# Coefficient loads reordered, down stages two slots later, and query products handled as pairs

## The chip, the cores and the metric

The kernel runs on one core of a Trainium2 chip. The metric is the time of one execution on the device in microseconds; times before are the median of three runs. One execution was also profiled, and all rows come from it. The page abbreviates the engines: PE is TensorE's products and PEld its weight loads, DVE is VectorE, ACT is ScalarE, POOL is GpSimd, SP is SyncE, and a q behind a name (SPq) is the engine's own instruction queue.

## What is computed

One transformer layer with linear attention and a butterfly feed-forward part, x being 4 x 1024 x 128 in fp32, with 16 heads of 64:

```python
qkv = x @ W_qkv                               # 128 -> 3 * 1024
fmap = lambda t: relu(t @ W_f + b_f)          # per head, 64 x 64
q, k = fmap(q), fmap(k)
kv = einsum('bhnd,bhne->bhde', k, v)
out = einsum('bhnd,bhde->bhne', q, kv)
normalizer = einsum('bhnd,bhd->bhn', q, k.sum(axis=2))
out = out / (normalizer[..., None] + 1e-06)
x = layernorm(x + out @ W_out + b_out)
h = butterfly(x @ W_exp + b_exp, up_weights, 512)       # 9 stages
h = butterfly(gelu(h + up_bias), down_weights, 512)     # 9 stages
x = layernorm(x + h @ W_con + b_con + down_bias)
```

A butterfly stage takes each pair of features whose indices differ in one bit and multiplies it by a 2 x 2 matrix of its own. All stages are linear, so the kernel applies them to the weights once and not to each token.

## The kernel before

Each engine runs a program of its own, with semaphores between them. After a prologue that loads and folds weights, the work is laid out over 48 slots (`for s in range(SLOTS)`, in every engine's program, and always in the order written there); what belongs to slot s is given by small tables and functions at the head of the kernel. An engine works through its own list in order, so an operation that waits holds up all behind it on that engine, the next slots too.

The main stream, in the order in which a unit goes through it:

- **k tiles** (`k_tiles`, 32 of 128 tokens: two a slot in slots 0 to 3, then one a slot to slot 27). TensorE projects a tile in two halves, ScalarE copies each through a ReLU into `k`, TensorE multiplies the tile with x (`add_kx`), and VectorE adds it to `k_total` (`k_sum`).
- **k sums**: after a batch's eight tiles TensorE reduces `k_total` over tokens (`ksum`, slots 6, 14, 22, 30) into the PSUM bank `desk`, and VectorE spreads the result by `ksum_mask` into `ksum_cols`, its first operation in that slot. All later transposes and head maps go through the same bank, so the next of them waits for that.
- **q products** (`q_steps`, 64 of 128x512, two a slot in slots 4 to 35): TensorE, then ScalarE's ReLU into the ring `q` of 16 (`q_relu`).
- **normalizers**: every 4th slot from 8 on, `norm` on TensorE, `norm_eps` on ScalarE, `reciprocal` on VectorE; SyncE's `spread(n)` then writes the reciprocals to DRAM and reads them back broadcast over partitions, in two halves, into `recips`. The first `spread` stands in SyncE's program behind all loads of coefficients.
- **normalised q** (`spreads`, two a slot in slots 10 to 41): VectorE multiplies q by the reciprocals (`normalise_q`, into `qn`, two buffers), ScalarE copies it in the reduced format fp32r (`qn_hi`, into `qn_h`), VectorE subtracts that copy for the low part (`qn_lo`, into `qn_l`); in the next slot TensorE adds the three products of `add_attn` (slots 11 to 42).
- **attention end**: `transpose_attn`, then in slots 15, 19, ... 43 VectorE's `add_x` and layer norm. GpSimd makes the reciprocal deviation (`rstd_of`), and VectorE's `layer_norm_end` waits for it.
- **feed-forward**: up products with GELU, `down`, `transpose_y`, and VectorE's `residual` with a second layer norm, in slots 22, 26, ... 42, 44, 47.

Beside that stream the two butterflies are applied to the weights. GpSimd does the nine up stages (`up_step`, on `y_up`) ahead of its slots, three operations each. VectorE does the nine down stages (`down_step`, on `y_dn`), two products and a sum each, stage n in slot 1 + n (`DOWN_STEP_SLOT`), as the last large operation of the slot; besides there are small stages for the biases (`bias_row_step`, slots 2 to 5). The results are wanted in slot 15. A stage's coefficients are 512 KB, broadcast to all partitions by SyncE's `load_up(n)` and `load_down(n)` into two buffers each. From n = 2 on a load waits for both products of stage n - 2 to be done (`s_up` or `s_dn` at 3n - 4), and SyncE issues all its transfers in order.

The lines of VectorE's slot that the change touches, of the kernel before:

```python
for a in spreads(s):
    normalise_q(a)
if s in NORM_SLOT:
    reciprocal(NORM_SLOT[s])
# xT_lo, x1T_lo, k_sum of this slot
for a in spreads(s)[:1]:
    qn_lo(a)
# add_x or residual of this slot, with the statistics of its layer norm
for a in spreads(s)[1:]:
    qn_lo(a)
# layer_norm_end, m_lo, down_step
```

Of the kernel before, what the change touches and what calls it, by code (L numbers as in the profile page):

```python
# [5 lines left out]
def postln_linear_attention_butterfly_ffn_kernel(  # L6
# [52 lines left out]
    QRING = 16  # L59
# [51 lines left out]
    WEIGHTS_SLOT = 15  # L111
    DOWN_STEP_SLOT = {1 + n: n for n in range(STAGES)}

# [48 lines left out]
    with ctx:  # L162
# [169 lines left out]
        def _(sp):  # L332
# [36 lines left out]
            load_up(0)  # L369
            load_down(0)  # L370
            sp.dma_start(xs[1][:, :, :], xs_view[1, :, :, :]).then_inc(s_xs[1], 16)
            load_down(1)
            load_up(1)
            sp.dma_start(coef_rows[:, :, :], up_weights[0:LOCAL, :, :, :].rearrange("s (a k) i j -> a s (k i j)", a=HT))\
                .then_inc(s_ccol, 16)
            for st in range(LOCAL, STAGES):
                sp.dma_start(coef_cols[:, st - LOCAL, :, :],
                             up_weights[st, :, :, :].rearrange("(m p) i j -> p m (i j)", p=128)).then_inc(s_ccol, 16)
            column(bout_col[:, :], b_out)
            column(bcon_col[:, :], b_con)  # L380
            column(bdn_raw[:, :], down_bias)
            for i in range(HT):
                column(bup_raw[:, i:i + 1], up_bias[i * 128:(i + 1) * 128])
            for n in range(2, STAGES):
                load_down(n)
                load_up(n)
                if n == 4:
                    for b in range(2, BATCH):
                        sp.dma_start(xs[b][:, :, :], xs_view[b, :, :, :]).then_inc(s_xs[b], 16)

            def spread(n):

                sp.wait_ge(s_r, n + 1)
                for j in range(4):
                    sp.dma_start(recip_rows[n, :, j * QT:(j + 1) * QT], recip[32 * j:32 * j + 2 * PAIRS, :])\
                        .then_inc(s_rst, 16)
                sp.wait_ge(s_rst, 64 * (n + 1))
                rows = recip_rows[n, :, :].rearrange("(o p h) t -> h o p t", o=1, h=2)
                for half in range(2):
                    g = 2 * n + half  # L400
                    if g >= 2:
                        sp.wait_ge(s_qn, RC * (g - 1))
                    for h in range(2):
                        sp.dma_start(recips[h * D:(h + 1) * D, half, :, :],
                                     rows[h, :, half * RC:(half + 1) * RC, :].to_broadcast([D, RC, CH]))\
                            .then_inc(s_rc[half], 16)
# [71 lines left out]
        def _(pe):  # L478
# [115 lines left out]
            def add_attn(a):  # L594
# [3 lines left out]
                if p == 0 and a:  # L598
                    pe.wait_ge(s_atc, a // PAIRS)
                pe.wait_ge(s_qnh, a + 1)  # L600
                pe.wait_ge(s_qnl, a + 1)
                split(attn_ps[:, :], (m_h[:, p, :], m_l[:, p, :]), (qn_h[:, a % NRING, :], qn_l[:, a % NRING, :]),
# [140 lines left out]
        def _(act):  # L743
# [17 lines left out]
            def q_relu(i):  # L761
                act.wait_ge(s_made, ring_of["q", i] + 1)
                if i >= QRING:
                    act.wait_ge(s_qn, i - QRING + 1)
                a_.activation(q[:, i % QRING, :], bank(("q", i))[:, :], ACT.Relu, bias=bf_col[:, :])\  # L765
                    .then_inc(s_taken, 1)

            def qn_hi(a):
                act.wait_ge(s_qn, a + 1)
                if a >= NRING:  # L770
                    act.wait_ge(s_at, a - NRING + 1)
                hi(qn_h[:, a % NRING, :], qn[:, a % 2, :], s_qnh)

# [69 lines left out]
            for s in range(SLOTS):  # L843
# [6 lines left out]
                if s == 0:  # L850
                    for half, fold in enumerate([attn_ps, spare_ps]):
                        act.wait_ge(s_fold, half + 3)
                        hi(wq_h[:, half * CH:(half + 1) * CH], fold[:, :], s_wh)
                for a in spreads(s)[:1]:
                    qn_hi(a)
                for i in q_steps(s)[:1]:
                    q_relu(i)
                for kt in k_tiles(s)[:1]:
                    k_relu(kt, 1)
                for a in spreads(s)[1:]:  # L860
                    qn_hi(a)
                for n in range(ALLCH):
# [34 lines left out]
        def _(dve):  # L897
# [91 lines left out]
            def normalise_q(a):  # L989
                if a % RC == 0:  # L990
                    dve.wait_ge(s_rc[a // RC % 2], 32 * (a // RC // 2 + 1))
                if a >= 2:
                    dve.wait_ge(s_qnh, a - 1)
                    dve.wait_ge(s_qnl, a - 1)
                v.tensor_tensor(qn[:, a % 2, :], q[:, a % QRING, :], recips[:, a // RC % 2, a % RC, :],  # L995
                                ALU.mult).then_inc(s_qn, 1)

            def qn_lo(a):
                dve.wait_ge(s_qnh, a + 1)
                lo(qn_l[:, a % NRING, :], qn[:, a % 2, :], qn_h[:, a % NRING, :], s_qnl)  # L1000

# [59 lines left out]
            for s in range(SLOTS):  # L1061
# [4 lines left out]
                if s == 0:  # L1066
                    for half, fold in enumerate([attn_ps, spare_ps]):
                        cols = slice(half * CH, (half + 1) * CH)
                        dve.wait_ge(s_wh, 3 + half)
                        lo(wq_l[:, cols], fold[:, :], wq_h[:, cols], s_wl)  # L1070
                for a in spreads(s):
                    normalise_q(a)
# [13 lines left out]
                if s in YT_SLOT:  # L1086
                    residual(YT_SLOT[s])
                for a in spreads(s)[1:]:
                    qn_lo(a)
                if s in ATT_T_SLOT:  # L1090
# [56 lines left out]
```

## Time and profile before

| | |
|---|---|
| median of three runs | 380.69 us (380.1 to 384.87) |
| the profiled execution's own time | 380.9 us, of which 379.0 are the span of the profile |
| TensorE products, busy | 333.4 us (88% of the span) |
| VectorE, busy | 246.2 us (65%) |
| ScalarE, busy | 173.0 us (46%) |
| GpSimd, busy | 80.6 us (21%) |
| mean granted clock of TensorE | 0.938 of full |

The rows that follow in their own section are of three kinds. A page line gives totals. A table by stage gives for each stretch of time how long each engine was busy in it, and the clock that TensorE was granted. The order of time of one engine gives each operation's start and duration, with the idle time ahead of it and who ended that idle time in brackets. Records of operations that follow each other overlap a little, so starts are the surer measure.

### The profile page before, as it was taken

The numbers are of one execution on the slowest core, as the hardware profiler recorded it, in microseconds if no ns is written. First come the engines' busy times: TensorE is split into PE (matmuls) and PEld (weight loads), VectorE is DVE, ScalarE is ACT, GpSimd is POOL, SyncE is SP. The second block draws the span as 40 slices with busy tenths as digits, with TensorE's granted clock in tenths as the row PEclk, the third lists the DMA queues.
The fourth block names the chain that finished last, engine by engine and source line by source line (L and its number), as shares of the span: only waits on it lengthen the run. The fifth ranks groups of instructions, "written<-read, shape, count | busy, mean of one in ns | idle before, by whom it ended". The sixth has DMA issues, their size and how long they took to land.

```text
span 379.0 us, 5158 instructions
## 1 busy us (share of the span) xinstructions
PE 333.4 (88%) x1841; PEld 235.3 (62%) x1841; DVE 246.2 (65%) x489; ACT 173.0 (46%) x289; POOL 80.6 (21%) x77
## 2 busy tenths in 40 slices
PE   4898999299799999999999999999979788589481
PEld 3765677176567767777767675776856565356250
DVE  3536999999956384666518774685585783882613
ACT  2531344034455564674645464646546543434120
POOL 3080565896300002001001100110110110111201
PEclk9999999879989999999999999999999989659766
DMA  5940509333902800630450046006505607500000
GB/s 176 302 143 32 191 17 315 113 112 117 214 9 48 179 0 2 149 78 2 112 115 0 2 110 144 2 3 139 113 2 123 132 3 164 116 0 0 29 28 28
DMA packets 25089, 33.73 MB, mean 89 GB/s; under 512 B 3656, under 2 KB 13928, under 8 KB 25064
## 3 DMA queue, kind: packets, MB, share of 16 engines
q1 hardware_dynamic: 24904, 33.38, 34.6%
q8 instruction: 14, 0.23, 0.2%
q14 instruction: 11, 0.09, 0.1%
q10 hardware_dynamic: 160, 0.03, 0.0%
HBM read 31.04 MB, written 2.36 MB: 88 GB/s over the span
## 4 chain that ended last, share of the span: by engine, by line
PE 52%; DVE 28%; issue 7%; DMA 6%; POOL 4%; ACT 2%; SPq 1%; POOLq 0%; DVEq 0%
PE ring L483 18%; PE kx_ps L555 9%; PE attn_ps L483 8%; DVE late L914 6%; PE ring L643 5%; DMA recips<-recip_rows 4%; DVE qn L995 3%; POOL rstd L462 3%; DVE stats L1004 3%; PE ring L535 2%; PE ring L575 2%; DVE bias_row_term L930 2%; PE desk L492 2%; DVE k_total L969 2%; DVE y_dn L918 2%
## 5 line engine op out<-in xcount | busy, mean ns | idle before, releaser
L765 ACT ACTIVATE q<-ring,bf_col 128x512 f32<-128x512 f32 x64 | 43.9, 686 | 52.3 <-PE ring L483 51.9
L555 PE MATMUL kx_ps<-k,xs 128*128 128x512 f32 x128 | 60.2, 593 | 0.8 <-ACT k L758 0.8
L751 ACT ACTIVATE qn_h<-qn 128x512 fp32r<-128x512 f32 x64 | 39.8, 627 | 36.7 <-DVE qn L995 36.7
L758 ACT ACTIVATE k<-ring 128x512 f32<-128x512 f32 x64 | 38.3, 598 | 34.2 <-PE ring L535 33.8
L901 DVE TENSOR_TENSOR qn_l<-qn,qn_h 128x512 fp32r<-128x512 f32 x64 | 42.9, 680 | 15.8 <-ACT qn_h L751 15.0
L459 POOL TENSOR_TENSOR var_eps<-mean_var,ln_eps 128x4 f32<-128x4 f32 x16 | 7.1, 443 | 205.0 <-DVE mean_var L1008 205.0
L995 DVE TENSOR_TENSOR qn<-q,recips 128x512 f32<-128x512 f32 x64 | 41.1, 684 | 10.5 <-DMA recips<-recip_rows 10.5
L451 POOL TENSOR_TENSOR y<-hid,y_up 128x512 f32<-128x512 f32 x18 | 38.3, 2150 | 39.8 <-DMA hid<-in_L_ffn_up_weights_dram 39.7
L555 PEld LDWEIGHTS kx_ps<-k,xs 128*128 128x128 f32 x128 | 24.1, 189 | 19.2 <-issue 16.5
L483 PE MATMUL ring<-xT_h,wq_h 128*128 128x512 f32 x64 | 35.9, 561 | 0.0
L483 PE MATMUL attn_ps<-qn_h,m_h 128*128 128x512 f32 x64 | 29.2, 456 | 7.6 <-DVE qn_l L901 3.9
L969 DVE TENSOR_TENSOR k_total<-k_total,k 128x1024 f32<-128x1024 f32 x24 | 32.3, 1347 | 0.8 <-ACT k L758 0.6
L483 PE MATMUL ring<-wk_h,xT_h 128*128 128x512 f32 x64 | 29.7, 464 | 3.0 <-ACT q L765 2.0
L643 PE MATMUL ring<-hid,wdn 128*128 128x512 f32 x64 | 30.3, 618 | 0.0
L483 PE MATMUL attn_ps<-qn_l,m_h 128*128 128x512 f32 x64 | 26.7, 417 | 0.0
L483 PE MATMUL attn_ps<-qn_h,m_l 128*128 128x512 f32 x64 | 26.6, 416 | 0.0
L817 ACT ACTIVATE hid<-ring,bup_col 128x512 f32<-128x512 f32 x32 | 22.0, 686 | 9.0 <-PE ring L483 8.8
L483 PE MATMUL ring<-wk_l,xT_h 128*128 128x512 f32 x64 | 25.8, 403 | 0.0
L483 PE MATMUL ring<-wk_h,xT_l 128*128 128x512 f32 x64 | 25.8, 403 | 0.0
L535 PE MATMUL ring<-bf_rows,ones_r 128*128 128x512 f32 x64 | 25.6, 400 | 0.0
L483 PE MATMUL ring<-xT_h,wq_l 128*128 128x512 f32 x64 | 25.5, 399 | 0.0
L483 PE MATMUL ring<-xT_l,wq_h 128*128 128x512 f32 x64 | 25.4, 396 | 0.0
(125 smaller groups left out, 549.7 us busy)
## 6 DMA issues: line engine op xcount, KB each, us to landing
recips<-recip_rows SPq DMA_DIRECT2D x32, 512.0 KB, 7.3
hid<-in_L_ffn_up_weights_dram SPq DMA_DIRECT2D x9, 512.0 KB, 5.3
x<-_L_ffn_down_weights_dram SPq DMA_DIRECT2D x9, 512.0 KB, 4.1
xs<-in_L_attn_x_dram SPq DMA_DIRECT2D x4, 512.0 KB, 7.4
out_dram<-y SPq DMA_DIRECT2D x8, 256.0 KB, 6.1
q<-in_L_attn_W_qkv_dram SPq DMA_DIRECT2D x2, 512.0 KB, 7.9
q<-in_L_attn_W_qkv_dram SPq DMA_DIRECT2D x2, 256.0 KB, 3.3
q<-in_L_attn_W_out_dram SPq DMA_DIRECT2D x2, 256.0 KB, 8.8
```

The source lines that it names most:

```text
L451: g.tensor_tensor(term_up[f].rearrange("p (hi j lo) -> p hi j lo", j=2, lo=lo), w[:, :, :, :, f], yv[:, :, f:f + 1, :].to_broadcast([128, ...
L483: last = t_.matmul(dst, lhsT, rhs, start=start and n == 0, stop=stop and n == len(pairs) - 1)
L535: t_.matmul(dst, ones_r[:, :], bf_rows[:, :], start=False, stop=True).then_inc(s_made, 1)
L555: t_.matmul(kx_ps[half], xs[b % XBUF][:, t, :], k[kt % KRING][:, half * CH:(half + 1) * CH], start=t == 0, stop=t == TILES - 1).then_inc(s ...
L643: last = t_.matmul(bank(("down", n))[:, :], wdn[:, i, :], hid[:, i, :], start=i == 0, stop=i == HT - 1)
L751: a_.activation(dst, src, ACT.Copy).then_inc(done, 1)
L758: a_.activation(k[kt % KRING][:, half * CH:(half + 1) * CH], bank(("k", kt, half))[:, :], ACT.Relu).then_inc(s_taken, 1)
L765: a_.activation(q[:, i % QRING, :], bank(("q", i))[:, :], ACT.Relu, bias=bf_col[:, :])\
L901: v.tensor_tensor(dst, src, high.bitcast(fp32), ALU.subtract).then_inc(done, 1)
L914: v.tensor_tensor(term_dn[j].rearrange("p (hi f lo) -> p hi f lo", f=2, lo=lo), w[:, :, j, :, :], yv[:, :, j:j + 1, :].to_broadcast([128, ...
L969: v.tensor_tensor(k_total[:, :], k_total[:, :], k[kt % KRING][:, :], ALU.add).then_inc(s_ks, 1)
L995: v.tensor_tensor(qn[:, a % 2, :], q[:, a % QRING, :], recips[:, a // RC % 2, a % RC, :], ALU.mult).then_inc(s_qn, 1)
```

## The change

Four edits, all of them in the order or the grouping of work; what is computed stays the same.

1. SyncE's loads. Before: up 0, down 0, x of batch 1, down 1, up 1, the bias coefficients and columns, then down n and up n by turns for n = 2 to 8, with x of batches 2 and 3 after n = 4. After: up 0, up 1, x of batch 1, bias coefficients, up 2, down 0, the columns, up 3, down 1, x of batches 2 and 3, up 4, 5, 6, down 2, up 7, down 3, up 8, down 4, then down 5 to 8.
2. Down stage n is done in slot 3 + n and not 1 + n.
3. `normalise_q`, `qn_hi` and `qn_lo` work on both q products of a slot as one operation of 128x1024. `qn` holds one pair, and the semaphores count pairs. `qn_lo` stands where the first one stood, ahead of `add_x` and `residual`; the second one, behind them, is gone.
4. On ScalarE `qn_hi` now stands behind the first `q_relu` of the slot and not ahead of it.

```diff
-    DOWN_STEP_SLOT = {1 + n: n for n in range(STAGES)}
+    DOWN_STEP_SLOT = {3 + n: n for n in range(STAGES)}
...
             load_up(0)
-            load_down(0)
+            load_up(1)
             sp.dma_start(xs[1][:, :, :], xs_view[1, :, :, :]).then_inc(s_xs[1], 16)
-            load_down(1)
-            load_up(1)
...
+            load_up(2)
+            load_down(0)
             column(bout_col[:, :], b_out)
...
-            for n in range(2, STAGES):
+            load_up(3)
+            load_down(1)
+            for b in range(2, BATCH):
+                sp.dma_start(xs[b][:, :, :], xs_view[b, :, :, :]).then_inc(s_xs[b], 16)
+
+            for n in range(4, STAGES):
+                load_up(n)
+                if n >= 6:
+                    load_down(n - 4)
+            for n in range(STAGES - 4, STAGES):
                 load_down(n)
-                load_up(n)
-                if n == 4:
-                    for b in range(2, BATCH):
-                        sp.dma_start(xs[b][:, :, :], xs_view[b, :, :, :]).then_inc(s_xs[b], 16)
...
-                        sp.wait_ge(s_qn, RC * (g - 1))
+                        sp.wait_ge(s_qn, RC // 2 * (g - 1))
...
-                pe.wait_ge(s_qnh, a + 1)
-                pe.wait_ge(s_qnl, a + 1)
+                pe.wait_ge(s_qnh, a // 2 + 1)
+                pe.wait_ge(s_qnl, a // 2 + 1)
...
             def qn_hi(a):
-                act.wait_ge(s_qn, a + 1)
+                act.wait_ge(s_qn, a // 2 + 1)
                 if a >= NRING:
-                    act.wait_ge(s_at, a - NRING + 1)
-                hi(qn_h[:, a % NRING, :], qn[:, a % 2, :], s_qnh)
+                    act.wait_ge(s_at, a - NRING + 2)
+                hi(qn_h[:, a % NRING:a % NRING + 2, :], qn[:, :, :], s_qnh)
...
+                for i in q_steps(s)[:1]:
+                    q_relu(i)
                 for a in spreads(s)[:1]:
                     qn_hi(a)
-                for i in q_steps(s)[:1]:
-                    q_relu(i)
                 for kt in k_tiles(s)[:1]:
                     k_relu(kt, 1)
-                for a in spreads(s)[1:]:
-                    qn_hi(a)
...
-                v.tensor_tensor(qn[:, a % 2, :], q[:, a % QRING, :], recips[:, a // RC % 2, a % RC, :],
-                                ALU.mult).then_inc(s_qn, 1)
+                v.tensor_tensor(qn[:, :, :], q[:, a % QRING:a % QRING + 2, :],
+                                recips[:, a // RC % 2, a % RC:a % RC + 2, :], ALU.mult).then_inc(s_qn, 1)
 
             def qn_lo(a):
-                dve.wait_ge(s_qnh, a + 1)
-                lo(qn_l[:, a % NRING, :], qn[:, a % 2, :], qn_h[:, a % NRING, :], s_qnl)
+                dve.wait_ge(s_qnh, a // 2 + 1)
+                pair = slice(a % NRING, a % NRING + 2)
+                lo(qn_l[:, pair, :], qn[:, :, :], qn_h[:, pair, :], s_qnl)
...
-                for a in spreads(s):
+                for a in spreads(s)[:1]:
                     normalise_q(a)
...
-                for a in spreads(s)[1:]:
-                    qn_lo(a)
```

## Rows read from the trace of the kernel before

**Rows 1.** The page, busy time of each engine, share of the span, instructions.

```profile
PE 333.4 (88%) x1841; PEld 235.3 (62%) x1841; DVE 246.2 (65%) x489; ACT 173.0 (46%) x289; POOL 80.6 (21%) x77
```

**Rows 2.** Table by stage: from:to, length, busy us by engine, clock, DMA.

```profile
67.50:74.67 7.17, 0.15 (x1) 0.00 (x0) 7.10 (x8) 0.69 (x1) 6.58 (x4) 0.87 0.41 146
74.67:80.00 5.33, 5.33 (x16) 4.36 (x17) 5.29 (x5) 1.88 (x3) 5.33 (x2) 0.53 0.24 65
...
105.60:200.00 94.40, 94.40 (x591) 68.38 (x590) 52.79 (x98) 52.00 (x88) 4.03 (x5) 0.99 0.31 69
...
268.00:337.00 69.00, 56.26 (x353) 40.26 (x352) 48.85 (x135) 31.94 (x56) 9.36 (x12) 0.89 0.36 81
```

**Rows 3.** Order of time, TensorE: start, duration, operation, [idle before <- releaser].

```profile
74.67 1.11 PE L492 MATMUL desk<-ident,xs 128*128 128x128 f32 x4 [7.02 <-DVE ksum_cols L975]
...
94.84 1.09 PE L589 MATMUL desk<-vo,kx 128*64 128x128 f32 x16
...
103.54 0.80 PE L483 MATMUL ring<-wk_h,xT_h 128*128 128x512 f32 x1 [2.04 <-ACT q L765]
...
105.42 0.63 PE L483 MATMUL attn_ps<-qn_h,m_h 128*128 128x512 f32 x1
...
209.48 0.66 PE L492 MATMUL desk<-ident,late 128*128 128x128 f32 x4 [0.62 <-DVE xT_l L901]
```

**Rows 4.** Order of time, VectorE, slots 1 to 10.

```profile
33.70 2.07 DVE L914 TENSOR_TENSOR late<-x,y_dn 128x512 f32<-128x512 f32 x2
...
55.18 0.69 DVE L918 TENSOR_TENSOR y_dn<-late 128x512 f32<-128x512 f32 x1
55.79 0.67 DVE L930 TENSOR_TENSOR bias_row_term<-coef_rows,bias_rows 4x128 f32<-4x128 f32 x2
56.49 0.28 DVE L934 TENSOR_TENSOR bias_rows<-bias_row_term 4x128 f32<-4x128 f32 x1
...
61.51 1.85 DVE L918 TENSOR_TENSOR y_dn<-late 128x512 f32<-128x512 f32 x1
...
101.57 1.28 DVE L995 TENSOR_TENSOR qn<-q,recips 128x512 f32<-128x512 f32 x2
```

**Rows 5.** Order of time, VectorE, slot 34, and slot 38's start.

```profile
294.82 1.30 DVE L995 TENSOR_TENSOR qn<-q,recips 128x512 f32<-128x512 f32 x2 [4.00 <-DMA recips<-recip_rows]
...
296.83 0.68 DVE L1029 TENSOR_TENSOR y<-desk,x 128x512 f32<-128x512 f32 x1
...
298.75 0.66 DVE L901 TENSOR_TENSOR qn_l<-qn,qn_h 128x512 fp32r<-128x512 f32 x1
300.58 1.12 DVE L1013 TENSOR_SCALAR y<-y,mean_var,rstd 128x128 f32<-128x128 f32 x4 [1.18 <-POOL rstd L462]
301.62 1.28 DVE L995 TENSOR_TENSOR qn<-q,recips 128x512 f32<-128x512 f32 x2
...
321.38 1.29 DVE L995 TENSOR_TENSOR qn<-q,recips 128x512 f32<-128x512 f32 x2 [6.10 <-DMA recips<-recip_rows]
```

**Rows 6.** Order of time, operations of 128x1024, and two copies of 128x512.

```profile
57.71 1.21 DVE L969 TENSOR_TENSOR k_total<-k_total,k 128x1024 f32<-128x1024 f32 x1
...
55.63 1.02 ACT L778 ACTIVATE kx<-kx_ps 128x1024 f32<-128x1024 f32 x1
...
309.99 1.14 ACT L751 ACTIVATE qn_h<-qn 128x512 fp32r<-128x512 f32 x2
```

**Rows 7.** Order of time, GpSimd, products of an up stage.

```profile
18.76 2.56 POOL L451 TENSOR_TENSOR y<-hid,y_up 128x512 f32<-128x512 f32 x2 [13.84 <-DMA hid<-in_L_ffn_up_weights_dram]
...
60.88 3.87 POOL L451 TENSOR_TENSOR y<-hid,y_up 128x512 f32<-128x512 f32 x2 [7.61 <-DMA hid<-in_L_ffn_up_weights_dram]
```

**Rows 8.** Order of time, SyncE's queue: stores and reads of the reciprocals.

```profile
91.10 1.73 SPq L395 DMA_DIRECT2D recip_rows<-recip  x4
93.87 2.56 SPq L404 DMA_DIRECT2D recips<-recip_rows  x4
...
313.91 2.56 SPq L404 DMA_DIRECT2D recips<-recip_rows  x4
```

More of the change, by code:

```diff
@@ L763, in q_relu @@
                 if i >= QRING:
-                    act.wait_ge(s_qn, i - QRING + 1)
+                    act.wait_ge(s_qn, (i - QRING) // 2 + 1)
                 a_.activation(q[:, i % QRING, :], bank(("q", i))[:, :], ACT.Relu, bias=bf_col[:, :])\
@@ L991, in normalise_q @@
                     dve.wait_ge(s_rc[a // RC % 2], 32 * (a // RC // 2 + 1))
-                if a >= 2:
-                    dve.wait_ge(s_qnh, a - 1)
-                    dve.wait_ge(s_qnl, a - 1)
-                v.tensor_tensor(qn[:, a % 2, :], q[:, a % QRING, :], recips[:, a // RC % 2, a % RC, :],
-                                ALU.mult).then_inc(s_qn, 1)
+                if a:
+                    dve.wait_ge(s_qnh, a // 2)
+                    dve.wait_ge(s_qnl, a // 2)
+                v.tensor_tensor(qn[:, :, :], q[:, a % QRING:a % QRING + 2, :],
+                                recips[:, a // RC % 2, a % RC:a % RC + 2, :], ALU.mult).then_inc(s_qn, 1)
             def qn_lo(a):
-                dve.wait_ge(s_qnh, a + 1)
-                lo(qn_l[:, a % NRING, :], qn[:, a % 2, :], qn_h[:, a % NRING, :], s_qnl)
+                dve.wait_ge(s_qnh, a // 2 + 1)
+                pair = slice(a % NRING, a % NRING + 2)
+                lo(qn_l[:, pair, :], qn[:, :, :], qn_h[:, pair, :], s_qnl)
             def layer_norm(i, n, src):
```

## The prediction

> **What bounds the kernel now.** I read the page's busy shares first, then a table by stage, then the order of time of single engines with what each waits for. TensorE is busy for 333 of 379.0 us, so it is the first suspect [rows 1]. The table by stage tells where it isn't the bound: from 67.5 to 74.67 us it is all but idle while VectorE is full; from 105.6 to 200 it is full while VectorE has 53 of 94 us of work; from 268 to 337 it is busy for 56 of 69 us, and no other engine is full either [rows 2]. So there are three stages.
>
> Stage one, to 105.6 us: TensorE's one long wait, 7.0 us, is for `ksum_cols` in slot 6, a VectorE operation that stands behind the down stages and bias stages of slots 1 to 5 [rows 3]. After it the granted clock is 0.53 to 80 us, near the 1.2 GHz level, after 7 us with nearly no work: 5.3 us at half the clock, so up to 2.5 us lost [rows 2]. A second wait, 2.0 us, ends at 103.54, when ScalarE has been released by the first normalise at 101.57 [rows 3, 4]. Stage two is TensorE's, and a delay that reaches it is passed on whole; VectorE is late for it once only, 0.62 us at 209.48 [rows 3]. Stage three is a chain through VectorE, ScalarE and GpSimd: two slots with a layer norm, a reciprocal, the DMA of the reciprocals, and again. A layer-norm slot there lasts from 294.82 to 301.62, 6.8 us [rows 5]. Six lie on that chain: slots 30, 31, 34, 35, 38 and 39.
>
> **The pairs, in the layer-norm slots.** Before, VectorE does the first low part as soon as ScalarE has copied the first of two products, and the residual add starts 2.01 us after the first normalise (294.82 to 296.83). The second low part stands behind the statistics, in the wait for GpSimd's `rstd`, of which 1.18 us stay idle even so [rows 5]: its 0.66 us are free. After, three operations of double length stand in series ahead of the add. A VectorE operation of 128x1024 in SBUF takes 1.21 us; a ScalarE copy of 128x1024 takes 1.02 from PSUM, and two of 512 from SBUF 1.14 [rows 6]. I take 1.21 + 1.02 + 1.21, and let two handovers of 0.03 and the 0.08 by which VectorE's next operation overlaps (300.58 plus 1.12 against 301.62) cancel nearly: 3.42 in the place of 2.01, +1.41 a slot. Bounds: 1.55 with the copy at 1.14, 1.3 if all three overlap as much. The low part leaves a place where it was free, and the wait for `rstd` grows by 0.6. Six slots: +8.5. In slot 30 the copy also stands behind a ReLU of q that TensorE makes only after that slot has begun: an estimate of +0.4. In slot 40, without a layer norm, the attention products wait for both low parts in the same way: +1.3. Together **+10.2 us**, bounds 7.8 and 11.
>
> In slots 32, 33, 36 and 37 a longer chain lies under the DMA of the reciprocals, for which VectorE idled 4.0 and 6.1 us [rows 5]: nothing. In stage two TensorE needs the low parts only in the next slot, with some 5 us of its own products between: nothing, but for slot 22. There the residual add comes later by about 1.1 us (0.5 for the pair's copy and 0.6 for the second low part moved ahead; the sum of a k tile covers the rest), and `xT_l` in slot 23, for which TensorE already waits [rows 3], comes later by as much: **+1.1**.
>
> One rule speaks for the pairs. By the Trainium skill, VectorE: DVE Perf Modes, the section on the TRN2 errata, an operation that reads SBUF pays a fixed extra latency, so one large tile pays once where small ones pay each time. The rows bear out a small part of it: 1.21 against 1.28 for two, and 1.02 against 1.14. Were all 32 triples on the path, it would bring 32 x (2 x 0.07 + 0.12), some 8 us.
>
> **The loads and the down stages.** A down stage is two products, 2.07 us, and a sum, 0.69, some 2.7 us; a bias stage is 0.67 + 0.28, with gaps 0.98 [rows 4]. Each GpSimd operation that runs meanwhile holds VectorE up by about 1.16 us: a sum took 0.69 at 55.18, and 1.85 at 61.51 with GpSimd at work since 60.88 [rows 4, 7]. Two down stages (5.4 us) leave the work ahead of `ksum_cols`: stages 0 to 2, in slots 3 to 5, stand there instead of 0 to 4. Up stages 2 to 6 no longer wait for the down stages' coefficients; an up stage is three operations of 1.28 [rows 7], and by my count they are done by 50 us, for the most part while VectorE has little to do. But `load_down(2)` now waits for the products of down stage 0 in slot 3, and `load_up(7)` stands behind it in SyncE's queue, as `load_up(8)` does behind `load_down(3)`. So up stages 7 and 8 run at about 58 and 65 us, and hold VectorE up six times.
> VectorE from about 56.6, when its copy of `vo` in slot 4 is done (TensorE's slots up to there are as before): down 1, two bias stages, down 2, one bias stage 8.3 us and six holds 7.0, then `ksum_cols` done at 72 less the last hold that it may escape: about 71. TensorE waits 3.6 us instead of 7.0, and its clock would still have fallen. The second half of slot 9's head maps, which ends at 95.9 before [rows 3], comes at 92.3, or 89.8 with the clock kept.
>
> **Where that gain goes.** SyncE issues in order. `load_down(8)` waits for the products of down stage 6. Before, that was in slot 7, ahead of the reciprocals of slot 8, which went out at 91.10 as soon as they were there [rows 8]. Now stage 6 stands in slot 9, behind `m_l`, which waits for the head maps' products and their copy. So: maps 92.3, copy 0.65, `m_l` 0.65, two products 2.07, issue of the load 0.4: the reciprocals leave at 96.1. From their first store to the first read's issue are 2.77 us, from that to the normalise 7.4 (313.91 to 321.38) [rows 5, 8]: 106.3 in the place of 101.57. Queued behind that normalise are the k sum of slot 10, the low parts and down stages 7 and 8, and on ScalarE the pair's copy and the k and q copies that free TensorE's banks. The first attention product comes 3.4 us later, at 109.7 against 105.42 [rows 3]: **+4.3 us**. Bounds: with `ksum_cols` taken at once and the clock kept (9.5 us earlier) -1; with no relief at all +8, and 1.5 more for a clock that stays low longer. Down stages 7 and 8 (4.5 us) then lie beside 14 us of TensorE's work in slots 11 and 12: nothing. The earlier loads of `xs` 2 and 3, the later columns and the waits counted in pairs cost nothing: their first readers come some slots later.
>
> **Sum.** 10.2 + 1.1 + 4.3 = 15.6 on the profiled execution's own 380.9, which is the shown median (380.69) within 0.1%: 396.5 us.
>
> **Rivals.**
> A, above, both losses: 392 to 402, chance 0.53.
> B, the tail is lost but the reciprocals aren't late, since `ksum_cols` is taken at once and the clock kept: 380.9 + 11.3 - 1 = 391 (387 to 392). For it: VectorE now idles in slots 1 and 2. Against: six GpSimd operations fall just ahead of slot 6. 0.20.
> C, the pair is covered in the layer-norm slots and the front loses 4.3: 385. Only if the residual add waits for TensorE's transposes and not for the low part; the rows show no idle time ahead of the add [rows 5]. 0.09.
> D, the pairs pay by the fixed part that each saves, and the rest cancels: 1 to 8 us less, about 376. 0.04. The errata section named above is the rule for it.
> E, the other side: VectorE's relief ahead of slot 6 goes through to TensorE. It is worth 7.0 us of wait, 2.5 of slow clock and 2.0 at 103.54: 369. It needs the first normalise ten microseconds earlier, so reciprocals out by 81, and stage 6's place in SyncE's queue forbids that unless slot 9 ends before; and it decides only where the relief is larger than the tail's 11. 0.08.
> F, no relief in slot 6 and the late reciprocals in full: 380.9 + 11.3 + 8 + 1.5 = 402 and above. 0.06.
>
> The range, 386 to 404, leaves out C's low part, D and E; the likeliest case's own is 392 to 402. About 2% is what a measurement of this kernel tells from no change (373 to 388.3): slower is A, F and most of B, 0.77; the same is C, D and the rest, 0.15; faster is E, 0.08.
>
> **What would show it.** In the changed profile a layer-norm slot near 300 us has the normalise, one copy and one low part in series, the add 3.4 us after the normalise, and a wait for `rstd` of 1.8 us. The waits show VectorE's `qn` behind the DMA of the reciprocals near 100 us, for some 9 us, and TensorE's behind `ksum_cols` halved. I am wrong if the add comes within 2.3 us, if the first store of reciprocals leaves before 91, or if both show and the end moves less than 6 us: then there is a slack between that I don't see.

## The result, and the profile after

| | before | changed |
| --- | --- | --- |
| median | 381.08 us (380.1 to 384.87, 4 runs) | 405.2 us (404.51 to 405.91, 4 runs) |
| ratio | | 1.061, 95% interval 1.054 to 1.069 |
| span of the profile | 379.0 us | 404.1 us |

The change makes the kernel 24.1 us slower; 396.5 had been predicted, with 386 to 404 as the range. The sign and both places of the loss were right, the size was not. A few executions come out over 1.5% longer than the fastest of the same kernel: the medians and ratios of the experiments leave them out, c1's trace, which is of such a one, is not used, and g1's is read only up to slot 30. Lining up operations of the two traces gives where the 25.1 us between the spans arise:

| place | start before | start after | delay so far |
| --- | --- | --- | --- |
| `ksum_cols`, slot 6 | 74.22 | 75.08 | 0.9 |
| first store of reciprocals | 91.10 | 100.73 | 9.6 |
| first normalise | 101.57 | 112.07 | 10.5 |
| first attention product | 105.42 | 115.79 | 10.4 |
| key sums on TensorE (`ksum`), slot 22 | 197.58 | 210.19 | 12.6 |
| transposes, slot 23 | 209.48 | 222.69 | 13.2 |
| normalise, slot 34 | 294.82 | 311.18 | 16.4 |
| normalise, slot 38 | 321.38 | 342.65 | 21.3 |
| end of the span | 379.0 | 404.1 | 25.1 |

So 12.6 us are lost in the front, 0.6 in slot 23, 11.9 from slot 30 on.

**The front.** TensorE of the changed kernel, in order of time (columns as in [rows 3]):

```profile
62.60 2.49 PE L569 MATMUL desk<-ones,k_total 128*128 128x1 f32 x16 [0.85 <-DVE k_total L972]
...
75.53 1.12 PE L497 MATMUL desk<-ident,xs 128*128 128x128 f32 x4 [3.63 <-DVE ksum_cols L978]
...
95.83 1.09 PE L594 MATMUL desk<-vo,kx 128*64 128x128 f32 x16
...
115.79 0.76 PE L488 MATMUL attn_ps<-qn_h,m_h 128*128 128x512 f32 x1 [12.38 <-DVE qn_l L904]
...
222.69 0.66 PE L497 MATMUL desk<-ident,late 128*128 128x128 f32 x4 [1.23 <-DVE xT_l L904]
```

The wait for `ksum_cols` is halved, 3.63 us in the place of 7.02 [rows 3], yet the head maps come 1 us later than before: `ksum_cols` itself is 0.9 us later, and TensorE reached that wait at 71.90 instead of 67.65. The table by stage says why TensorE was late (columns as in [rows 2]):

```profile
62.60:70.65 8.05, 8.05 (x27) 5.84 (x28) 7.88 (x13) 1.86 (x3) 1.12 (x2) 0.58 0.34 134
70.65:75.53 4.88, 1.25 (x5) 0.54 (x3) 4.85 (x6) 0.69 (x1) 4.28 (x3) 0.84 0.31 107
75.53:80.85 5.32, 5.32 (x15) 4.35 (x16) 5.29 (x6) 1.88 (x3) 0.00 (x0) 0.50 0.23 72
...
103.41:115.79 12.38, 0.00 (x1) 0.03 (x1) 3.72 (x4) 2.46 (x4) 0.00 (x0) 0.69 0.78 171
115.79:123.00 7.21, 7.21 (x18) 5.21 (x18) 6.12 (x7) 2.87 (x5) 0.00 (x0) 0.58 0.00 0
```

After the 0.85 us wait at 62.60 the clock is near its lower level for 8 us, after the 3.63 us wait again for 5, and after 12.38 idle microseconds again for 7. VectorE and GpSimd around `ksum_cols`, and VectorE and SyncE around the reciprocals:

```profile
54.71 1.92 DVE L933 TENSOR_TENSOR bias_row_term<-coef_rows,bias_rows 4x128 f32<-4x128 f32 x2
...
62.39 0.67 DVE L1110 COPY vo<-spare_ps 128x512 f32<-128x512 f32 x1
...
70.67 3.15 DVE L933 TENSOR_TENSOR bias_row_term<-coef_rows,bias_rows 4x128 f32<-4x128 f32 x2
...
75.08 0.40 DVE L978 TENSOR_TENSOR ksum_cols<-head_mask,desk 128x256 f32<-128x256 f32 x1
...
87.11 0.95 DVE L984 RECIPROCAL recip<-recip 128x128 f32<-128x128 f32 x1 [2.23 <-ACT recip L803]
...
97.60 0.69 DVE L904 TENSOR_TENSOR m_l<-desk,m_h 128x512 fp32r<-128x512 f32 x1 [4.65 <-ACT m_h L756]
98.21 2.12 DVE L917 TENSOR_TENSOR late<-x,y_dn 128x512 f32<-128x512 f32 x2
...
112.07 1.22 DVE L998 TENSOR_TENSOR qn<-q,recips 128x1024 f32<-128x1024 f32 x1 [11.01 <-DMA recips<-recip_rows]
```

```profile
52.17 4.00 POOL L456 TENSOR_TENSOR y<-hid,y_up 128x512 f32<-128x512 f32 x2
...
58.09 3.08 POOL L456 TENSOR_TENSOR y<-hid,y_up 128x512 f32<-128x512 f32 x2 [0.35 <-DMA hid<-in_L_ffn_up_weights_dram]
...
70.52 3.14 POOL L456 TENSOR_TENSOR y<-hid,y_up 128x512 f32<-128x512 f32 x2 [6.93 <-DMA hid<-in_L_ffn_up_weights_dram]
```

```profile
70.05 30.63 SPq L367 DMA_DIRECT2D x<-_L_ffn_down_weights_dram  x5
100.73 1.82 SPq L400 DMA_DIRECT2D recip_rows<-recip  x4
104.80 2.56 SPq L409 DMA_DIRECT2D recips<-recip_rows  x4
```

The reciprocals are ready at 88.1. Their first store goes out at 100.73, 12.7 us later and right behind the last load of down coefficients, which waited for the products of down stage 6 (98.21 and 2.12). Before, they were ready at 91.08 and left at 91.10. Two bias operations that take 0.67 us together alone [rows 4] take 1.92 and 3.15 beside GpSimd.

**The layer-norm slots.** VectorE in slot 38 of the changed kernel, which answers to [rows 5]:

```profile
342.65 1.23 DVE L998 TENSOR_TENSOR qn<-q,recips 128x1024 f32<-128x1024 f32 x1 [5.20 <-DMA recips<-recip_rows]
344.99 1.23 DVE L904 TENSOR_TENSOR qn_l<-qn,qn_h 128x1024 fp32r<-128x1024 f32 x1 [1.12 <-ACT qn_h L756]
346.14 0.68 DVE L1033 TENSOR_TENSOR y<-desk,x 128x512 f32<-128x512 f32 x1
...
349.54 1.11 DVE L1017 TENSOR_SCALAR y<-y,mean_var,rstd 128x128 f32<-128x128 f32 x4 [1.40 <-POOL rstd L467]
350.57 1.22 DVE L998 TENSOR_TENSOR qn<-q,recips 128x1024 f32<-128x1024 f32 x1
```

The add comes 3.49 us after the normalise where it came 2.01 after, and the slot takes 7.92 us instead of 6.80. Slot 34 takes 9.69, since the pair's copy stands behind the copy of q there (ScalarE):

```profile
313.62 0.69 ACT L770 ACTIVATE q<-ring,bf_col 128x512 f32<-128x512 f32 x1 [0.70 <-PE ring L488]
314.21 1.05 ACT L756 ACTIVATE qn_h<-qn 128x1024 fp32r<-128x1024 f32 x1
```

### The profile page after: what moved, and what is told of

Its sections match the earlier page's. It is cut to its first block, busy times and chain, and to the rows that moved or that the text cites. A ratio compares the mean times of both kernels' runs of the same rounds, so it can differ in the third digit from the quotient of the medians.

```text
span 404.1 us, 5001 instructions
## 1 busy us (share of the span) xinstructions
PE 340.8 (84%) x1841; PEld 240.3 (59%) x1841; DVE 241.1 (60%) x425; ACT 168.7 (42%) x257; POOL 71.6 (18%) x77
## 4 chain that ended last, share of the span: by engine, by line
PE 63%; DVE 19%; DMA 6%; issue 4%; ACT 3%; POOL 3%; SPq 1%; POOLq 0%; DVEq 0%; ACTq 0%
PE ring L488 23%; PE kx_ps L560 12%; PE attn_ps L488 9%; PE ring L648 6%; PE ring L580 3%; DMA recips<-recip_rows 3%; PE ring L540 3%; PE desk L497 3%; DVE late L917 2%; ACT qn_h L756 2%; POOL rstd L467 2%; PE desk L594 2%; DVE stats L1008 2%; DVE qn_l L904 2%; DVE qn L998 2%
## 5 line engine op out<-in xcount | busy, mean ns | idle before, releaser
L560 PE MATMUL kx_ps<-k,xs 128*128 128x512 f32 x128 | 61.6, 604 | 0.8 <-ACT k L763 0.8
L904 DVE TENSOR_TENSOR qn_l<-qn,qn_h 128x1024 fp32r<-128x1024 f32 x32 | 39.2, 1224 | 35.4 <-ACT qn_h L756 35.3
L756 ACT ACTIVATE qn_h<-qn 128x1024 fp32r<-128x1024 f32 x32 | 33.7, 1052 | 41.1 <-DVE qn L998 41.1
L998 DVE TENSOR_TENSOR qn<-q,recips 128x1024 f32<-128x1024 f32 x32 | 39.0, 1220 | 19.2 <-DMA recips<-recip_rows 18.2
L464 POOL TENSOR_TENSOR var_eps<-mean_var,ln_eps 128x4 f32<-128x4 f32 x16 | 3.2, 200 | 221.4 <-DVE mean_var L1012 221.4
L560 PEld LDWEIGHTS kx_ps<-k,xs 128*128 128x128 f32 x128 | 25.0, 196 | 20.0 <-issue 17.1
L456 POOL TENSOR_TENSOR y<-hid,y_up 128x512 f32<-128x512 f32 x18 | 32.0, 1801 | 21.9 <-DMA hid<-in_L_ffn_up_weights_dram 21.1
L972 DVE TENSOR_TENSOR k_total<-k_total,k 128x1024 f32<-128x1024 f32 x24 | 33.3, 1386 | 0.3
L488 PEld LDWEIGHTS attn_ps<-qn_h,m_h 128*128 128x128 f32 x64 | 13.0, 204 | 32.9 <-issue 25.6
```

Of the source, the lines that this page charges most:

```text
L456: g.tensor_tensor(term_up[f].rearrange("p (hi j lo) -> p hi j lo", j=2, lo=lo), w[:, :, :, :, f], yv[:, :, f:f + 1, :].to_broadcast([128, ...
L488: last = t_.matmul(dst, lhsT, rhs, start=start and n == 0, stop=stop and n == len(pairs) - 1)
L560: t_.matmul(kx_ps[half], xs[b % XBUF][:, t, :], k[kt % KRING][:, half * CH:(half + 1) * CH], start=t == 0, stop=t == TILES - 1).then_inc(s ...
L756: a_.activation(dst, src, ACT.Copy).then_inc(done, 1)
L904: v.tensor_tensor(dst, src, high.bitcast(fp32), ALU.subtract).then_inc(done, 1)
L972: v.tensor_tensor(k_total[:, :], k_total[:, :], k[kt % KRING][:, :], ALU.add).then_inc(s_ks, 1)
```

## The experiments

Twelve kernels in four groups. The kernel before was run beside each group: its medians were 379.68 (first four), 378.76 (next four), 378.11 (next three) and 380.44 us (last). Ratios are to it, with 95% intervals. "Edit 1" to "edit 4" are those of the change's own list.

### The edits apart

c1 has edits 1 and 2, c2 edits 3 and 4, c3 edit 2, c4 edit 1; their diffs are the parts of the one shown.

> The changed load order and down stages in slots 3 to 11, with q products singly as before. Theory: the first 12.5 us of the loss come from these two edits (reciprocals held behind the last down load in SyncE's queue), the rest from the pairs. So first store of reciprocals at 100 to 101 us, first normalise at 112, end 10 to 12.5 us after before: 391 to 393. The layer-norm slots near the end last 6.8 us as before. Rival: the late low parts of the pairs make the front loss too; then the end is within 5 us of before, 386 or less.

> Pairs and ScalarE's new order alone, loads and down stages as before. Theory: 11 to 13 us slower, 392 to 393.5, all of it from slot 22 on: 0.6 in slot 23, the rest in slots 30 to 40, with 7.9 us for a layer-norm slot in the place of 6.8. The front is as before within 1 us. Rival: the two losses share a cause (TensorE late in the tail since it was late in front); then pairs alone cost under 8 us, below 389.

> Down stage n in slot 3 + n, load order as before, so up stages wait for the down stages' loads. Theory (the queue makes the loss): reciprocals leave at about 100 us as in the changed kernel, end 9 to 12 us after before, 390 to 393. Rival (GpSimd's early up stages eat the relief by holding VectorE): with fewer up stages ahead of slot 6 the relief shows, ksum_cols by 69 to 72 us in the place of 74.2, and the end only 4 to 7 us after before, 385 to 388.

> The changed load order alone, down stages in slots 1 to 9. Reciprocals then are not held, since stage 6 stands in slot 7. Queue theory alone: the first normalise stays near 101.6 us and the end within 2 us of before. Rival (holds): all up stages run before about 65 us and hold VectorE some nine times more ahead of slot 6, ksum_cols near 84 us, TensorE waits 15 us or more for it, end 5 to 8 us after before, 386 to 389.

| kernel | edits | median | ratio | over before |
| --- | --- | --- | --- | --- |
| c1 | 1, 2 | 390.93 | 1.029 (1.019 to 1.039) | 11.3 |
| c2 | 3, 4 | 392.52 | 1.035 (1.028 to 1.042) | 12.8 |
| c3 | 2 | 391.44 | 1.032 (1.025 to 1.040) | 11.8 |
| c4 | 1 | 381.02 | 1.005 (1.002 to 1.009) | 1.3 |
| changed | all | 405.2 | 1.061 (1.054 to 1.069) | 24.1 |

The two halves add up: 11.3 and 12.8 against 24.1. The front's whole loss is edit 2's; the reordered loads cost 1 to 2 us alone. c3, VectorE and SyncE:

```profile
88.54 4.54 DVE L914 TENSOR_TENSOR late<-x,y_dn 128x512 f32<-128x512 f32 x2
...
95.80 0.68 DVE L901 TENSOR_TENSOR m_l<-desk,m_h 128x512 fp32r<-128x512 f32 x1
96.40 2.10 DVE L914 TENSOR_TENSOR late<-x,y_dn 128x512 f32<-128x512 f32 x2
...
112.13 1.29 DVE L995 TENSOR_TENSOR qn<-q,recips 128x512 f32<-128x512 f32 x2 [12.90 <-DMA recips<-recip_rows]
```

```profile
98.53 0.33 SPq L367 DMA_DIRECT2D x<-_L_ffn_down_weights_dram  x1
98.90 0.43 SPq L361 DMA_DIRECT2D hid<-in_L_ffn_up_weights_dram  x1
99.37 1.81 SPq L395 DMA_DIRECT2D recip_rows<-recip  x4
104.76 2.57 SPq L404 DMA_DIRECT2D recips<-recip_rows  x4
```

Here `ksum_cols` came at 70.69, 3.5 us earlier than before; the relief by two down stages is real, and the second half of the head maps starts at 90.58, 4.3 us earlier. None of it arrives, since the store again stands behind the last load, which waits for stage 6's products. Here it is not the head maps that make stage 6 late but VectorE itself, held by the up stages: stage 5's products at 88.54 take 4.54 us instead of 2.04. In c4 `ksum_cols` came at 80.83, 6.6 us later than before, since down stages 0 to 4, whose coefficients now come later, all still stand ahead of it. Yet the end moved by 1 to 2 us only: the first store left at 91.49, nearly as before. For the end it is the store's time that counts.

### The store's place, and GpSimd's holds

e1 is the changed kernel with the last load of down coefficients behind the first reciprocals. e2 is the changed kernel with GpSimd's up stages 5 to 8 on 4 of 512 columns, which leaves out most of the up weights' last four stages.

```diff
-            for n in range(STAGES - 4, STAGES):
+            for n in range(STAGES - 4, STAGES - 1):
                 load_down(n)
...
                     spread(n)
+                if n == 0:
+                    load_down(STAGES - 1)
```

> The changed kernel, with the last down load put behind the first spread in SyncE's program. Theory (the queue makes the front loss): the store of the reciprocals leaves at about 88 us, as soon as they are made, and not at 100.7; the first normalise comes when VectorE is free, at about 101, the first attention product at about 105, and the end 11 to 13 us before the changed kernel's: 392 to 394. Rival: VectorE's late work behind slot 6, not the queue, sets the first attention product; then the end gains less than 4 us, above 401.

> The changed kernel with GpSimd's up stages 5 to 8 done on 4 of 512 columns (that part of the up weights is left out). Theory (holds eat the relief): without some ten operations that hold VectorE for 1.16 us each, ksum_cols is made at about 64 us, before TensorE asks for it at 67.5; head maps, down stage 6 and the reciprocals come 8 to 10 us earlier, the first normalise at 102 to 104, the end at 395 to 397. Rival (holds cost little, the stages of biases and copies make the queue): ksum_cols stays above 70 and the end moves less than 4 us.

| | `ksum_cols` | first store | first normalise | median | ratio |
| --- | --- | --- | --- | --- | --- |
| changed | 75.08 | 100.73 | 112.07 | 405.2 | 1.061 |
| e1 | 73.70 | 89.74 | 101.54 | 392.74 | 1.035 (1.030 to 1.040) |
| e2 | 64.20 | 89.58 | 101.31 | 393.56 | 1.038 (1.032 to 1.044) |

Either one takes back the front's loss whole; what is left, 14.0 and 14.8 us over the kernel before, is c2's loss or little more, and the three intervals overlap. e1 gives the cause without leaving anything out: one load moved behind the store is worth 12.4 us between the spans (404.1 and 391.7), as was expected of it. e2 shows the other condition (its end came out 1.4 us under the expected 395 to 397). Without the holds `ksum_cols` is 10.9 us earlier, the head maps at 84.68, stage 6 at 87.06, and the queue frees at 89.6. But more it does not bring, though TensorE is ahead by ten microseconds: it then waits 12.77 us for the first attention product, because the store still stands behind stage 6. The late store needs both, the load in the queue and a late stage 6, be it by late head maps as here or by a held VectorE as in c3.

### The pair against the single

e3 is the kernel before with its second low part moved ahead of the add, products still single. e4 is c2 with the pair's copy ahead of the copy of q, as before (edit 3 without edit 4).

```diff
-                for a in spreads(s)[:1]:
+                for a in spreads(s):
                     qn_lo(a)
...
-                for a in spreads(s)[1:]:
-                    qn_lo(a)
```

> The kernel before, with the second low part of a slot moved ahead of add_x and residual; single operations as before. It parts the place of the low part from the length of the pair. Theory: the add comes 0.6 us later (2.6 after the normalise), but GpSimd's variance operation, no longer behind a low part, is 0.35 shorter: 0.25 a slot in six slots and 0.6 in slot 23, in all 1 to 3 us slower, 382 to 384. Rival: the place is most of the pairs' cost; then 387 or more.

> Pairs alone, with ScalarE's copy ahead of the first q ReLU as before. Theory: the ReLU ahead of the copy costs only where TensorE makes that q product late, in slots 30 and 34: 2 to 3 us, so 389.5 to 391 against 392.5 with the new order. Rival: the order costs nothing or helps; 392.5 or more.

e3: 385.84 us, ratio 1.018 (1.014 to 1.022), 7.1 us over before; between the two expectations. VectorE of e3, slot 30:

```profile
270.10 1.28 DVE L995 TENSOR_TENSOR qn<-q,recips 128x512 f32<-128x512 f32 x2
271.48 0.69 DVE L901 TENSOR_TENSOR qn_l<-qn,qn_h 128x512 fp32r<-128x512 f32 x1
272.58 0.69 DVE L901 TENSOR_TENSOR qn_l<-qn,qn_h 128x512 fp32r<-128x512 f32 x1 [0.40 <-ACT qn_h L751]
273.19 0.68 DVE L1029 TENSOR_TENSOR y<-desk,x 128x512 f32<-128x512 f32 x1
```

The add is 3.09 us after the normalise: 0.6 for the low part, 0.5 for its copy, which stands behind the copy of q. That slot takes 7.52 us; slots 38 and 39, without q products, take 7.03. So about half of the pairs' loss (7.1 of 12.8 us by the medians, 5.1 of 10.8 by the spans) is the low part moved ahead of the add. The rest comes from the merging itself: in slots 38 and 39 of c2, which take 7.93 us, one copy of double length stands where the first copy ran beside the second product. e4: 391.77 us, ratio 1.033 (1.028 to 1.038), 13.0 over before against c2's 12.8; the 2 to 3 us expected from the order were not there. Its slots 30 and 34 have no late copy and take 7.93 us each (8.42 and 8.53 in c2), but its slot 30 begins 0.9 us later than in c2, so the order of those two on ScalarE comes out even. The loss is edit 3's.

### The other way round

If the add's place sets the slot, putting it ahead of both low parts should gain. If the store's place sets the front, a schedule that keeps the queue free should let the relief through (rival E). f1 is the kernel before with the add first, f2 the kernel before rescheduled, f3 both, and g1 is f2 with up coefficients 7 and 8 loaded ahead of the first reciprocals.

```diff
# f1
-                for a in spreads(s)[:1]:
-                    qn_lo(a)
                 if s in ATT_T_SLOT:
                     add_x(ATT_T_SLOT[s])
                 if s in YT_SLOT:
                     residual(YT_SLOT[s])
-                for a in spreads(s)[1:]:
+                for a in spreads(s):
                     qn_lo(a)
```

```diff
# f2
-    DOWN_STEP_SLOT = {1 + n: n for n in range(STAGES)}
+    DOWN_STEP_SLOT = dict(zip([1, 2, 3, 6, 7, 8, 10, 11, 12], range(STAGES)))
...
-            for n in range(2, STAGES):
+            for n in range(2, STAGES - 2):
...
                     spread(n)
+                if n == 0:
+                    for m in range(STAGES - 2, STAGES):
+                        load_down(m)
+                        load_up(m)
```

> The kernel before, with the residual addition, the statistics that follow it on VectorE placed ahead of both low parts in each slot; nothing is left out. If the serial chain from one normalise to the next sets the slot of a layer-norm stage, the addition comes about 1.3 us after the normalise instead of 2.0, the low parts fill the 1.2 us for which VectorE waits for rstd, and each layer-norm slot takes about 6.1 to 6.3 us instead of 6.8: 9 such slots make 3 to 5 us, end at about 374 to 376 in the profile, ratio 0.985 to 0.992. The rival: the slot is set by the sum of VectorE's work or by TensorE, which gets its low parts later; then there is no change or a loss of up to 3 us.

> The kernel before, with another placement of stages alone (singles, down coefficients first as before): down stages in slots 1, 2, 3, 6, 7, 8, 10, 11, 12, and the loads of down and up coefficients 7 and 8 issued behind the first spread of reciprocals. Nothing is left out. If the 7 us for which TensorE waits for the key column sums is VectorE held by GpSimd and loaded with down stages 4 and 5, and the queue is kept free for the store of the reciprocals, the key column sums are ready at 67 or earlier, TensorE's wait goes, and the first normalise comes 8 to 11 us earlier than in the kernel before (at 91 to 94 instead of 101.6): end at 368 to 371, ratio 0.97 to 0.98. The rival: the front is set by GpSimd's own sequence or by the arrival of the weights, the gain of the wait is then given back before the first normalise, as with the down-first relief seen so far: within 2 us of the kernel before.

> Both of the foregoing edits together, nothing left out. They touch different stretches (front up to the first normalise, layer-norm slots), so the gains should add: 11 to 16 us, end at 363 to 368, ratio 0.955 to 0.972. If the front is set otherwise, only the 3 to 5 us of the layer-norm slots remain.

> The rescheduled kernel (down stages in slots 1, 2, 3, 6, 7, 8, 10, 11, 12), but only the down coefficients 7 and 8 are loaded behind the first reciprocals; the up coefficients 7 and 8 are loaded ahead of them. Nothing is left out. The rescheduled kernel had its first normalise 11.6 us earlier than the kernel before and kept 5.9 us of that at slot 30. If the rest was given back because GpSimd's up stages 7 and 8, from 97 to 109 us, held VectorE (low parts 3.74 and products of down stage 7 3.55 us) and TensorE then waited 3.0 and 0.8 us in slot 11 with a slow clock behind it, the waits near 111 go and slot 30 starts 3 to 5 us earlier: end at 366 to 368. The rival: VectorE's own work in slots 10 to 12, the down stages moved there, makes it late, held or not, or the up stages hold it as much at 85 to 95 ahead of the first normalise: then the end stays within 1.5 us of 370.9.

| kernel | median | ratio | span |
| --- | --- | --- | --- |
| f1 | 376.91 | 0.996 (0.992 to 0.999) | 375.4 |
| f2 | 372.71 | 0.985 (0.980 to 0.990) | 370.9 |
| f3 | 371.13 | 0.980 (0.974 to 0.985) | 370.5 |
| g1 | 376.97 | 0.987 (0.981 to 0.993) | 376.8 |

The medians lie 1.2 us (f1), 5.4 (f2), 7.0 (f3) and 3.5 (g1) under those of the kernel before in their groups.

f1: VectorE, slot 30:

```profile
268.57 1.28 DVE L995 TENSOR_TENSOR qn<-q,recips 128x512 f32<-128x512 f32 x2
270.18 0.69 DVE L1029 TENSOR_TENSOR y<-desk,x 128x512 f32<-128x512 f32 x1 [0.32 <-PE desk L492]
...
272.11 1.26 DVE L901 TENSOR_TENSOR qn_l<-qn,qn_h 128x512 fp32r<-128x512 f32 x2
274.27 1.12 DVE L1013 TENSOR_SCALAR y<-y,mean_var,rstd 128x128 f32<-128x128 f32 x4 [0.90 <-POOL rstd L462]
275.30 1.28 DVE L995 TENSOR_TENSOR qn<-q,recips 128x512 f32<-128x512 f32 x2
```

Here the add waits for the transposes, and the slot is 6.73 us; slots 31, 34, 38 and 39 take 6.32 or 6.33 where they took 6.8. That is under half a microsecond a slot and not 0.7: the wait for `rstd` is 0.9 still. Slot 36 begins 1.8 us earlier than before (307.18 against 308.99), slot 38 only 0.4 (321.02 against 321.38), for its reciprocals had 4.2 us from store to read and not 2.7. By the ratio 1.7 us are kept, 0.3 to 3.1, where 3 to 5 were expected: the mechanism shows in the slots, little of it at the end.

f2 lets the relief through as far as the first normalise, though at the end its ratio of 0.985 falls short of the 0.97 to 0.98 expected. TensorE has no wait and full clock at slot 6, `ksum_cols` comes at 65.78, and:

```profile
79.98 1.73 SPq L395 DMA_DIRECT2D recip_rows<-recip  x4
82.74 2.57 SPq L404 DMA_DIRECT2D recips<-recip_rows  x4
```

```profile
89.99 1.29 DVE L999 TENSOR_TENSOR qn<-q,recips 128x512 f32<-128x512 f32 x2 [1.59 <-DMA recips<-recip_rows]
...
104.30 3.55 DVE L918 TENSOR_TENSOR late<-x,y_dn 128x512 f32<-128x512 f32 x2
```

The normalise is 11.6 us earlier than before, the normalise of slot 30 only 5.9 (263.13 against 269.01). TensorE of f2 shows what stands between:

```profile
111.42 0.50 PE L487 MATMUL ring<-wk_h,xT_h 128*128 128x512 f32 x1 [2.96 <-ACT q L769]
113.41 0.76 PE L487 MATMUL attn_ps<-qn_h,m_h 128*128 128x512 f32 x1 [0.79 <-DVE qn_l L905]
```

GpSimd's up stages 7 and 8 run from 97 to 109 us, the products of down stage 7 take 3.55 us instead of 2.07 beside them, and the clock over 105 to 120 us is 0.77. g1 put this to the test: the two waits near 111 are gone, as expected, but the up loads now hold the store in the queue and the holds fall on the first normalise:

```profile
75.82 9.51 SPq L361 DMA_DIRECT2D hid<-in_L_ffn_up_weights_dram  x3
85.38 1.82 SPq L398 DMA_DIRECT2D recip_rows<-recip  x4
```

```profile
96.66 2.30 DVE L1001 TENSOR_TENSOR qn<-q,recips 128x512 f32<-128x512 f32 x2 [3.86 <-DMA recips<-recip_rows]
```

```profile
99.64 0.80 PE L489 MATMUL ring<-wk_h,xT_h 128*128 128x512 f32 x1 [5.58 <-ACT q L771]
```

One wait of 5.58 us takes the place of two of 3.75 together, and slot 30 begins at 265.81, 2.7 us later than in f2. So the expected 3 to 5 us were missed, by the rival's second form: the holds only moved. By the ratios g1 and f2 can't be told apart. f3 is the fastest kernel here, 1.5 to 2.6% under the kernel before, but its two gains do not add up as expected (11 to 16 us): over f2 it has 1.6 by medians and 0.4 by the spans.

## Why the prediction was right and wrong, point by point

**The bound of each stage: right.** A late reciprocal in the front and a longer layer-norm slot each came out whole at the end (c1, c2), and an earlier or later `ksum_cols` did not (c3, c4; 64.20 in e2 brought no more than 73.70 in e1). The page of the changed kernel would not have told: VectorE is less busy than before [rows 1], and the kernel slower.

```profile
PE 340.8 (84%) x1841; PEld 240.3 (59%) x1841; DVE 241.1 (60%) x425; ACT 168.7 (42%) x257; POOL 71.6 (18%) x77
```

**The queue, the term of +4.3 us: this is the step that failed.** Predicted 4.3 us, measured 12.6. That the store would be held behind the last load was right. The relief ahead of slot 6, which was to bring the head maps 3.6 us earlier and so to pay for most of that hold, was wrong: they came 1.0 us later. That TensorE's wait came out at 3.63 us, the 3.6 predicted, is chance, for it is halved because TensorE arrived 4.25 us late and not because `ksum_cols` came early. The steps from the head maps to the store held: copy, `m_l`, stage 6's products, issue, 3.8 us from the end of the maps predicted and 3.8 measured (96.92 to 100.73). The error came in at three places:

- *The relief ahead of slot 6, 4.6 us.* I started VectorE's count at 56.6, from its copy of `vo` "as before". That is the end of TensorE's product and 0.67 us; in the kernel before the copy is done only at 59.5, since VectorE comes to it late. Now it came at 62.39, done at 63.1, 6.4 us after my start, behind down stage 0 and two bias stages that GpSimd held from 50.8 on. From there to the end of `ksum_cols` it took 12.4 us and not the 14 to 15 of my sum, since most of the holds already lay behind. I had put up stages 2 to 6 "done by 50 us"; up stage 6 ran to 57.7, and 7 and 8 to 63.6 and 75.0. An up-stage product took 1.80 us in the mean of the changed kernel and not the 1.28 that I had counted; the kernel before already had 2.15 in the mean, and 3.87 for two in [rows 7]. GpSimd is held by VectorE as VectorE is by it. I counted six holds; ten GpSimd operations ran between 49.9 and 75.1 us. Head maps ended at 96.9 and not 92.3.
- *Store to read, 1.3 us.* 4.07 us in the place of 2.77 [rows 8]. In c3 it was 5.39, in e1 4.08, in g1 3.93, each with a load of coefficients just ahead of the store, and in f2 2.76 with none. But the last round of f1 took 4.2 and that of f3 4.6 with no load ahead, so the reason stays open.
- *The clock after the long idle time, 2.1 us.* The first attention product came 10.4 us late, slots 12 and beyond 12.5. After 12.38 idle microseconds the products stood 0.43 us apart for 7 us. I had this as a bound ("1.5 more for a clock that stays low longer") and left it out of the sum.

What happened is nearest to rival F, no relief at all, to which I gave 6 in 100 and 402 us "and above". Its 9.5 us for the front are still 3 short of the 12.6: the head maps came 1.0 us later than with no relief, store to read took 1.3 more, and the second slow stretch cost 2.1 in the place of 1.5.

By the Trainium skill, SBUF — State Buffer, the section on who interferes with whom, an operation of VectorE with both inputs in SBUF and one of GpSimd that reads SBUF exclude each other for a whole instruction, whichever is first. The rows agree, in both directions: 3.15 us for a pair of bias operations of 4x128 at 70.67 beside GpSimd, and GpSimd's mean of 1.80. The sum needs a count of both engines' operations in the same stretch, and that is what I had left out.

**Pairs in the layer-norm slots: right in mechanism, a little low.** Predicted 10.2 us, measured 11.9.

- The add: 3.42 us after the normalise predicted, 3.49 measured. Right.
- The slot: +1.41 predicted, +1.13 to 1.16 measured in slots 31, 35, 38 and 39. The wait for `rstd` was to grow by 0.6 to 1.8 and is 1.40. The 0.3 us came from GpSimd: `var_eps` takes 0.55 us in the kernel before, beside VectorE's second low part, and 0.20 after. The low part before was not all free; it cost 0.35.
- Slot 30, +0.4 beyond the slot's own, measured +0.5; slot 40, +1.3, measured +1.5. Right.
- Slot 34: nothing beyond the slot's own predicted, measured +1.8. The copy of q that the pair's copy stands behind (313.62) waited for TensorE in slot 34 too, behind down products. I had seen this in slot 30 only; with 1.2 us in smaller pieces between slots it is what was missing.
- Slot 23: +1.1 predicted, 0.6 measured.

**Rival D, the fixed part that each pair saves.** The rule of the Trainium skill that the prediction cites for it (VectorE: DVE Perf Modes, the section on the TRN2 errata) shows in the rows, in a small size. A pair saves 0.07 us on VectorE (1.22 against 1.28 or 1.29) and about 0.1 on ScalarE (1.05 against 1.14), and 64 VectorE operations fewer make its busy time 5 us less. None of that reached the end, as the prediction held: c2, which has all of it, is 12.8 us slower. e3 and f1 show that what counts is which operation stands ahead of the add, not how many there are.

**Rival E**, relief that goes through, did not happen and could not: its condition, the first store out by 81, is met only by f2 (79.98) and f3, which has f2's schedule.

## What to carry to other kernels

An operation that is moved later takes with it every load that waits for its buffer, and all that stands behind that load in an in-order DMA queue: look for a latency-bound store behind it before counting any relief, and put far-off prefetches behind it. Merging two operations saves their fixed part once, under 0.1 us here, and makes a chain of halves serial; on a chain through three engines it cost 12.8 us. Whether it pays where the engine itself is the bound, no run here shows. Where VectorE and GpSimd both work from SBUF, count the holds both ways, and lay out GpSimd's whole sequence in time first.

## What the runs showed of the hardware that I had not expected

- Small operations are held as well: GpSimd's `var_eps`, 128x4, takes 0.55 us with a VectorE low part beside it, 0.20 without. VectorE's 4x128 bias operations took up to 3.15 us a pair instead of 0.67.
- The granted clock fell near its lower level behind a wait of only 0.85 us, at 62.60, where TensorE then made 16 products of one column each: 0.58 over 8 us. Until 61.6 us products of 512 columns had stood 0.23 us apart. The one-column products alone did not do it: the kernel before made the same 16 at 61.68 without a wait, and its clock was 1.00 over 50 to 72.8 us.
- In the kernel before, the last attention products start at 337.17, behind a 0.53 us wait, and the clock over 337 to 348 us is 0.75. In f2 they start at 331.54 behind the same 0.53 us, and the clock over 332 to 340 is 1.00. From there to the end it is 41.8 us before and 39.4 in f2: of the 8.1 us between those two spans 2.4 arise in this stretch, where both make the same operations, and go with the clock. Why it rose earlier in the one than in the other stays open. Executions of one kernel differ in it too: beside f1 to f3 the kernel before took 376.73 us at a mean clock of 0.960 and 381.24 at 0.934. So a difference of some 2 us between two single traces says little of a schedule.
